# TensorE's order in a period of stage 1: the two fp32 products of a unit placed one on each side of the first tile's six products

## The chip, the cores and the metric

The kernel is one program on one core of a Trainium2 chip. TensorE does the matrix products, VectorE (DVE), ScalarE (ACT) and GpSimd (POOL) the work on elements, and SyncE (SP) issues the transfers between device memory and on-chip memory. The engines run side by side, each through its own instructions in the order written, and wait for each other at semaphores. The metric is the device time of one execution in microseconds (us). The median of three executions of the kernel before is 848.15 us (848.12 to 851.08).

## The reference

Two layers, one behind the other, for 32 sequences b of 128 channels and 2048 time steps:

```python
# layer 1: a session's own two-layer network, masked by channel and by length
W = W_sess[session_ids];  b = b_sess[session_ids]          # 128 x 256 for each sequence
h = einsum('bct,bch->bht', x * cmask, W) + b[:, :, None]
h = gelu(h)                                                # 256 hidden rows: two tiles of 128
out = (einsum('bht,hs->bst', h, W2) + b2) * tmask
# layer 2: a product in fp8, quantized with the largest magnitudes of out and of weight
w_q = fp8_e4m3(weight * w_scale);  x_q = fp8_e5m2(out * x_scale)
y = einsum('bsk,nk->bsn', x_q, w_q) / x_scale / w_scale + bias
return x + y
```

`x_scale` needs the largest magnitude of the whole `out`, so layer 2 can't begin before layer 1 has ended.

## The kernel before

The work has two stages. Stage 1 computes layer 1 for 64 units (half a sequence each: 128 channels x 1024 steps) and stores `out` to device memory; beside it the weight (128 x 32768 numbers) is scanned for its maximum (units 0 to 19) and later scaled, rounded and kept on chip in chunks of 768 columns. Stage 2 reads `out` back, quantizes it and makes the large product, 64 matmuls a sequence. The change touches stage 1 alone.

The hidden layer of a unit u has two tiles of 128 rows. Its precision comes from splitting: `xh` is x rounded to the fp32r format and `xl` the rest, `whl` holds the session weight's two parts, and `hidden(u, t)` (lines 698 to 722) makes tile t out of three products (weight high x `xh`, weight low x `xh`, weight high x `xl`), each in two halves of 512 columns: six matmuls, of one record each. `hidden(u, 0)` writes the first half of the tensor `ps_h` and `hidden(u, 1)` the second. Tile 0's output layer is split in the same way: `project0` (line 724) makes six matmuls of `w2h`, `w2l` with `hh` and `hl`. Tile 1's is `project1` (line 733): two products of unsplit fp32, one for each half, of which each has two records in the trace. Both add into `ps_o[:, u % 2]`.

The other engines, per unit, each in this order:

- ScalarE in its iteration u: `split_x(u + 2)` (line 448, writes `xh`), `gelu0(u + 1)` (lines 454 and 455: the gelu of tile 0 twice, once rounded into `hh`, once in place), in units 22 to 64 `scale_chunk` (line 471), `gelu1(u + 1)` (line 460, writes `h1`), and for 28 odd u `mask_session_weight` (line 478, writes `whl` for a later sequence). `split_x(u + 2)` waits until `hidden(u, 1)` has ended, `gelu0(u + 1)` until `hidden(u + 1, 0)` has, and `gelu1(u + 1)` until `hidden(u + 1, 1)` has.
- VectorE in its iteration u: `mask_o(u - 1)` (lines 567 and 570: bias and time mask out of `ps_o`, then the maximum), two operations on a weight chunk (lines 581 and 583) or, earlier, one part of the weight's scan (line 589), and `split_h_rest(u + 1)` (line 557: `hl`, what `hh` has left of the gelu), which stands ahead of the scan.
- GpSimd: `xl` (line 406), then the two rounding operations of a chunk (lines 413 and 415).

TensorE's order is written out by hand (lines 740 to 765). Its waits matter here: `hidden(u + 1, 0)` overwrites the half of `ps_h` that `hl` of unit u is computed from, so it waits for `hl_ready` of unit u. `hidden(u + 1, 1)` overwrites what `gelu1(u)` reads, and waits for `h1_gelu` of unit u, as the fp32 products do, which read `h1`. Every product into `ps_o` waits until VectorE has emptied that buffer two units earlier (`o_masked`).

Of the kernel before, what the change touches and what calls it, by code (L numbers as in the profile page):

```python
# [6 lines left out]
def adaln_ffn(nc, x, ids, lens, counts, w_sess, b_sess, w2, b2, weight, bias, out, masked_out, split_w):  # L7
# [8 lines left out]
    P = 128  # L16
    B, C, T = x.shape
    NSESS, _, HID = w_sess.shape
    HT = HID // P
    F = b2.shape[0] * 16  # L20
# [34 lines left out]
    HALVES = [slice(0, BANK), slice(BANK, UNIT)]  # L55
# [7 lines left out]
    with ExitStack() as ctx:  # L63
        def sb(name, shape, dt):
            return ctx.enter_context(nc.sbuf_tensor(name, shape, dt))

        def sem(name):
            return ctx.enter_context(nc.semaphore(name))
# [15 lines left out]
        w2_sb = sb("w2_sb", [P, HT, P], fp32)  # L84
        w2h = sb("w2h", [P, P], fp32r)
        w2l = sb("w2l", [P, P], fp32r)
# [21 lines left out]
        hh = sb("hh", [P, 2, UNIT], fp32r)  # L108
        hl = sb("hl", [P, 2, UNIT], fp32r)
        h1 = sb("h1", [P, 2, UNIT], fp32)  # L110
# [36 lines left out]
        ps_o = ctx.enter_context(nc.psum_tensor("ps_o", [P, 2, UNIT], fp32))  # L147
# [36 lines left out]
        h1_gelu = sem("h1_gelu")  # L184
        hl_ready = sem("hl_ready")
        o_psum = sem("o_psum")
        o_masked = sem("o_masked")
# [49 lines left out]
        def h0_of(u):  # L237

            return ps_o[:, 1, :] if u == 1 else ps_h[:, 0, :]
# [440 lines left out]
        def _(pe):  # L680
# [9 lines left out]
            def hidden_bias():  # L690
                pe.wait_ge(bs_loaded, 16)
                pe.wait_ge(onehot_ready, 1)
                for t in range(HT):
                    last_mm = nc.tensor.matmul(ps_o[:, 0, t * B:(t + 1) * B], bs_sb[:, t * P:(t + 1) * P],
                                               onehot[:, :], start=True, stop=True)
                last_mm.then_inc(hbias_psum, 1)

            def hidden(u, t):
                b = u // UPB
                to = h0_of(u) if t == 0 else ps_h[:, 1, :]  # L700
                if t == 0:
                    if u % UPB == 0:
                        if b < DIRECT:
                            pe.wait_ge(wh_direct, b + 1)
                        else:
                            pe.wait_ge(whl_masked, b - DIRECT + 1)
                    pe.wait_ge(xh_ready, u + 1)

                    if u > 1:
                        pe.wait_ge(hl_ready, u)  # L710
                elif u > 0:
                    pe.wait_ge(h1_gelu, u)
                for k, (part, xs) in enumerate(((0, xh), (1, xh), (0, xl))):
                    rows = slice(part * HID + t * P, part * HID + (t + 1) * P)
                    if k == 1 and t == 0 and b < DIRECT and u % UPB == 0:
                        pe.wait_ge(wl_direct, b + 1)
                    if k == 2 and t == 0:
                        pe.wait_ge(xl_ready, u + 1)
                    for cols in HALVES:
                        mm = nc.tensor.matmul(to[:, cols], whl[:, b % DIRECT, rows], xs[:, u % 2, cols],  # L720
                                              start=(k == 0), stop=(k == 2))
                mm.then_inc(h0_psum if t == 0 else h1_psum, 1)

            def project0(u, halves):

                pe.wait_ge(hl_ready, u + 1)
                if u >= 2:
                    pe.wait_ge(o_masked, u - 1)
                for k, (w, hs) in enumerate(((w2l, hh), (w2h, hh), (w2h, hl))):
                    for cols in halves:  # L730
                        nc.tensor.matmul(ps_o[:, u % 2, cols], w[:, :], hs[:, u % 2, cols], start=(k == 0), stop=False)  # L731

            def project1(u, halves):
                pe.wait_ge(h1_gelu, u + 1)
                for cols in halves:
                    mm = nc.tensor.matmul(ps_o[:, u % 2, cols], w2_sb[:, 1, :], h1[:, u % 2, cols],  # L736
                                          start=False, stop=True)
                mm.then_inc(o_psum, 1)

            hidden_bias()  # L740
            hidden(0, 0)
            hidden(0, 1)
# [2 lines left out]
            for u in range(UNITS - 2):  # L745
                if u > 0:
                    hidden(u + 1, 0)
                if u == SCANS + 2:

                    pe.wait_ge(scale_step, 1)  # L750
                project0(u, HALVES)
                if u == SCANS + 1:
                    pe.wait_ge(w_pmax_ready, 1)
                    nc.tensor.matmul(w_row, w_pmax, ident_f[:, :], start=True, stop=True).then_inc(w_row_psum, 1)
                hidden(u + 1, 1)
                project1(u, HALVES)
                if u == SCANS + 1:
                    pe.wait_ge(w_one_ready, 1)
                    nc.tensor.matmul(w_all, ones[:, :], w_one[:, :], start=True, stop=True).then_inc(w_amax_psum, 1)
# [22 lines left out]
            for k in range(CUTS):  # L782
                pe.wait_ge(q_ready, k + 1)
                pe.sem_inc(identity_turn, 1)
                for j in range(k * KT // CUTS, (k + 1) * KT // CUTS):
                    mm = nc.tensor.matmul(ps_q[:, j * P:(j + 1) * P], q_by_pair[:, 0, j // 2, :, j % 2], ident[:, :],
                                          start=True, stop=True)
# [50 lines left out]
```

## Time and profile before

| | |
|---|---|
| median of three executions | 848.15 us |
| profiled execution, its time | 847.79 us |
| its span, first to last instruction | 846.0 us |
| stage 1, until the last fp32 product | about 392 us |
| TensorE busy in the span | 832.6 us (98%) |
| TensorE busy at line 720, 731, 736 (stage 1) and 804 (stage 2) in the chain that ended last | 19%, 10%, 12% and 50% of the span |
| ScalarE, VectorE, GpSimd busy in the span | 320.1, 479.9, 444.2 us |
| TensorE's granted clock | 1.0 of full speed throughout |

In the profile's rows PE is a matmul on TensorE, PEld its weight load, which can run beside another matmul, and L720 a line of the kernel. Starts count from the first instruction. The end of a matmul is modelled, so lengths are better read from one start to the next. A bracket at the end of a row gives how long the engine had been idle before it and who released it.

### The profile page before, as it was taken

The numbers are of one execution on the slowest core, as the hardware profiler recorded it, in microseconds if no ns is written. First come the engines' busy times: TensorE is split into PE (matmuls) and PEld (weight loads), VectorE is DVE, ScalarE is ACT, GpSimd is POOL, SyncE is SP. The second block draws the span as 40 slices with busy tenths as digits, with TensorE's granted clock in tenths as the row PEclk, the third lists the DMA queues.
The fourth block names the chain that finished last, engine by engine and source line by source line (L and its number), as shares of the span: only waits on it lengthen the run. The fifth ranks groups of instructions, "written<-read, shape, count | busy, mean of one in ns | idle before, by whom it ended". The sixth has DMA issues, their size and how long they took to land.

```text
span 846.0 us, 9980 instructions
## 1 busy us (share of the span) xinstructions
PE 832.6 (98%) x3467; PEld 471.2 (56%) x3502; DVE 479.9 (57%) x495; ACT 320.1 (38%) x334; POOL 444.2 (53%) x195
## 2 busy tenths in 40 slices
PE   7999999999999999999999999999999999999998
PEld 4767676767767676675444444444444444444443
DVE  6889998888888888888532323232323232332322
ACT  5767777889888898884000000000000000000000
POOL 3634343799999999996632333323242424242321
PEclk9999999999999999999999999999999999999999
DMA  7799997676768866655569686867677676768672
GB/s 272 289 374 421 354 350 277 241 291 256 299 256 340 337 254 246 260 221 212 201 203 282 215 280 215 279 211 273 225 258 242 242 258 225 277 213 285 217 248 100
DMA packets 73022, 222.06 MB, mean 262 GB/s; under 512 B 37402, under 2 KB 39202, under 8 KB 52642
## 3 DMA queue, kind: packets, MB, share of 16 engines
q1 hardware_dynamic: 72994, 221.71, 73.1%
q8 instruction: 15, 0.25, 0.1%
q14 instruction: 13, 0.11, 0.0%
HBM read 144.35 MB, written 69.21 MB: 252 GB/s over the span
## 4 chain that ended last, share of the span: by engine, by line
PE 91%; DMA 3%; DVE 3%; issue 1%; POOL 1%; SPq 1%; ACT 1%; DVEq 0%
PE ps_h L804 50%; PE ps_h L720 19%; PE ps_o L736 12%; PE ps_o L731 10%; DMA split_w<-wqT 1%; DMA lens_i<-in_itok_B 1%; DVE hl L557 0%; DMA wraw<-split_w 0%; DMA x_sb<-x_sb 0%; DVE whl L523 0%; DVE x_sb L647 0%; DVE o_sb L567 0%; SPq L263 0%; POOL xl L406 0%; DVE wc L583 0%
## 5 line engine op out<-in xcount | busy, mean ns | idle before, releaser
L804 PE MATMUL ps_h<-wqT,x_sb 128*128 128x512 bf16 x2014 | 440.8, 379 | 2.7 <-DMA x_sb<-x_sb 0.8
L804 PEld LDWEIGHTS ps_h<-wqT,x_sb 128*128 128x128 fp8e5 x2048 | 200.1, 98 | 242.9 <-issue 2.2
L406 POOL TENSOR_TENSOR xl<-x_sb,xh 128x1024 fp32r<-128x1024 f32 x62 | 149.5, 2411 | 85.5 <-ACT xh L448 85.5
L720 PE MATMUL ps_h<-xh,whl 128*128 128x512 f32 x508 | 159.8, 436 | 3.6 <-DVE hl L557 2.4
L430 POOL TENSOR_TENSOR h<-h,bias_sb 128x2048 f32<-128x2048 f32 x16 | 73.3, 4579 | 139.0 <-DMA h<-in_x 139.0
L430 POOL TENSOR_TENSOR x_sb<-x_sb,bias_sb 128x2048 f32<-128x2048 f32 x16 | 72.3, 4519 | 139.9 <-DMA x_sb<-in_x 139.9
L670 DVE SCALAR_TENSOR_TENSOR o_sb<-ps_h,scales,h 128x512 f32<-128x512 f32 x64 | 48.0, 751 | 155.2 <-PE ps_h L804 155.2
L670 DVE SCALAR_TENSOR_TENSOR o_sb<-ps_h,scales,x_sb 128x512 f32<-128x512 f32 x64 | 47.8, 750 | 145.1 <-PE ps_h L804 145.1
L720 PEld LDWEIGHTS ps_h<-xh,whl 128*128 128x128 f32 x508 | 96.1, 190 | 51.6 <-issue 31.1
L736 PE MATMUL ps_o<-h,w_sb 128*128 128x512 f32 x256 | 120.3, 592 | 0.0
L567 DVE SCALAR_TENSOR_TENSOR o_sb<-ps_o,b_sb,steps 128x1024 f32<-128x1024 f32 (+1 forms) x65 | 82.2, 1265 | 32.0 <-PE ps_o L736 31.8
L454 ACT ACTIVATE hh<-ps_h,hbias 128x1024 fp32r<-128x1024 f32 x63 | 70.7, 1122 | 50.0 <-PE ps_h L720 50.0
L557 DVE TENSOR_TENSOR hl<-ps_h,hh 128x1024 fp32r<-128x1024 f32 x63 | 76.7, 1218 | 12.2 <-ACT ps_h L455 12.2
L720 PE MATMUL ps_h<-xl,whl 128*128 128x512 f32 x254 | 79.8, 395 | 0.0
L570 DVE TENSOR_REDUCE o_max<-o_sb 128x1 f32<-128x1024 f32 (+1 forms) x65 | 78.3, 1204 | 2.3
L460 ACT ACTIVATE h<-ps_h,hbias 128x1024 f32<-128x1024 f32 x64 | 71.3, 1114 | 17.0 <-PE ps_h L720 17.0
L413 POOL TENSOR_TENSOR ws<-ws,wc 128x768 f32<-128x768 f32 (+1 forms) x43 | 70.4, 1637 | 12.2 <-DVE wc L583 10.8
L415 POOL TENSOR_TENSOR wqT<-ws,wc 128x768 bf16<-128x768 f32 (+1 forms) x43 | 71.1, 1653 | 3.4
L736 PEld LDWEIGHTS ps_o<-h,w_sb 128*128 128x128 f32 x256 | 48.3, 189 | 36.2 <-issue 30.6
L455 ACT ACTIVATE ps_h<-ps_h,hbias 128x1024 f32<-128x1024 f32 x63 | 67.9, 1078 | 0.0
L448 ACT ACTIVATE xh<-x_sb 128x1024 fp32r<-128x1024 f32 x62 | 65.7, 1059 | 0.0
L720 PEld LDWEIGHTS ps_h<-xl,whl 128*128 128x128 f32 x254 | 48.1, 190 | 11.5 <-DVE xl L540 0.3
(79 smaller groups left out, 452.9 us busy)
## 6 DMA issues: line engine op xcount, KB each, us to landing
x_sb<-in_x SPq DMA_DIRECT2D x47, 1024.0 KB, 5.2
masked_out<-o_sb SPq DMA_DIRECT2D x32, 1024.0 KB, 5.4
o_in<-masked_out SPq DMA_DIRECT2D x32, 1024.0 KB, 8.9
out<-o_sb SPq DMA_DIRECT2D x31, 1024.0 KB, 5.1
h<-in_x SPq DMA_DIRECT2D x16, 1024.0 KB, 7.1
wt<-in_L_ffn_weight SPq DMA_DIRECT2D x42, 384.0 KB, 5.4
wqT<-in_L_ffn_weight SPq DMA_DIRECT2D x19, 832.0 KB, 8.1
wraw<-split_w SPq DMA_DIRECT2D x28, 256.0 KB, 5.0
```

Source lines behind the costliest of these rows:

```text
L406: pool.tensor_tensor(xl[:, u % 2, :], x_cols(u), xh[:, u % 2, :].bitcast(fp32), ALU.subtract)\
L415: pool.tensor_tensor(wqT[:, CHUNK_AT[i]], v, c, ALU.subtract).then_inc(w_rounded, 1)
L430: pool.tensor_tensor(x2[r], x2[r], bias_sb[:, :], ALU.add).then_inc(xb_ready, 1)
L460: act.activation(h1[:, u % 2, :], ps_h[:, 1, :], ACT.Gelu, bias=hbias[:, 1, b:b + 1])\
L557: dve.tensor_tensor(hl[:, u % 2, :], h0_of(u), hh[:, u % 2, :].bitcast(fp32), ALU.subtract)\
L567: dve.scalar_tensor_tensor(o_cols(u)[:, cols], ps_o[:, u % 2, cols], b2_sb[:, :], window, ALU.add, ALU.mult)\
L570: dve.tensor_reduce(o_max[:, u + k:u + k + 1], o_cols(u)[:, cols], AX.X, ALU.max, apply_absolute_value=True)\
L670: dve.scalar_tensor_tensor(y_sb[:, r, cols], ps_y[n], y_scale, x2[r][:, cols], ALU.mult, ALU.add).then_inc(y_ready, 1)
L720: mm = nc.tensor.matmul(to[:, cols], whl[:, b % DIRECT, rows], xs[:, u % 2, cols], start=(k == 0), stop=(k == 2))
L731: nc.tensor.matmul(ps_o[:, u % 2, cols], w[:, :], hs[:, u % 2, cols], start=(k == 0), stop=False)
L736: mm = nc.tensor.matmul(ps_o[:, u % 2, cols], w2_sb[:, 1, :], h1[:, u % 2, cols], start=False, stop=True)
L804: mm = nc.tensor.matmul(ps_y[n], qT[:, r, k // 2, :, k % 2], wq[:, n, k, :], start=(k == 0), stop=(k == KT - 1))
```

## The change

Inside the loop over the units, `project0` and `project1` are no longer called. The first fp32 product (`first_half`) now stands ahead of tile 0's six output products (`project`), the second (`second_half`) right behind them, and `hidden(u + 1, 1)` comes last in the loop's body. The wait for `h1_gelu` of unit u moves with the first fp32 product, and `ps_o` is started by it in its first half. The last two units, behind the loop, still call the old functions.

```diff
+            def first_half(u):
+                pe.wait_ge(h1_gelu, u + 1)
+                if u == 1:
+                    pe.wait_ge(hl_ready, u + 1)
+                if u >= 2:
+                    pe.wait_ge(o_masked, u - 1)
+                nc.tensor.matmul(ps_o[:, u % 2, HALVES[0]], w2_sb[:, 1, :], h1[:, u % 2, HALVES[0]], start=True, stop=False)
+
+            def project(u):
+                pe.wait_ge(hl_ready, u + 1)
+                for k, (w, hs) in enumerate(((w2l, hh), (w2h, hh), (w2h, hl))):
+                    for h, cols in enumerate(HALVES):
+                        mm = nc.tensor.matmul(ps_o[:, u % 2, cols], w[:, :], hs[:, u % 2, cols], start=(h == 1 and k == 0),
+                                              stop=(h == 0 and k == 2))
+                return mm
+
+            def second_half(u):
+                nc.tensor.matmul(ps_o[:, u % 2, HALVES[1]], w2_sb[:, 1, :], h1[:, u % 2, HALVES[1]], start=False, stop=True)\
+                  .then_inc(o_psum, 1)
...
-                project0(u, HALVES)
+                first_half(u)
+                project(u)
                 if u == SCANS + 1:
                     pe.wait_ge(w_pmax_ready, 1)
                     nc.tensor.matmul(w_row, w_pmax, ident_f[:, :], start=True, stop=True).then_inc(w_row_psum, 1)
+                second_half(u)
                 hidden(u + 1, 1)
-                project1(u, HALVES)
```

On TensorE in stage 1, one body of the loop of the kernel before, from the six products of `project0` to the next body's `hidden`. `w_sb` is W2 with `h` the array `h1`; L720 into `ps_h` is `hidden`, with one row for each wait:

```order
L731 MATMUL ps_o<-hh,w2l 128x512 [waits o_masked,hl_ready]
L731 MATMUL ps_o<-hh,w2l 128x512
L731 MATMUL ps_o<-hh,w2h 128x512 x2
L731 MATMUL ps_o<-hl,w2h 128x512 x2
L720 MATMUL ps_h<-xh,whl 128x512 [waits h1_gelu]
L720 MATMUL ps_h<-xh,whl 128x512 x3
L720 MATMUL ps_h<-xl,whl 128x512 x2
L736 MATMUL ps_o<-h,w_sb 128x512 [waits h1_gelu]
L736 MATMUL ps_o<-h,w_sb 128x512
L720 MATMUL ps_h<-xh,whl 128x512 [waits hl_ready,xh_ready,wh_direct]
```

The same stretch in the changed kernel, where L749 is `first_half`, L755 `project` and L761 `second_half`:

```order
L749 MATMUL ps_o<-h,w_sb 128x512 [waits o_masked,h1_gelu]
L755 MATMUL ps_o<-hh,w2l 128x512 [waits hl_ready]
L755 MATMUL ps_o<-hh,w2l 128x512
L755 MATMUL ps_o<-hh,w2h 128x512 x2
L755 MATMUL ps_o<-hl,w2h 128x512 x2
L761 MATMUL ps_o<-h,w_sb 128x512
L720 MATMUL ps_h<-xh,whl 128x512 [waits h1_gelu]
L720 MATMUL ps_h<-xh,whl 128x512 x3
L720 MATMUL ps_h<-xl,whl 128x512 x2
L720 MATMUL ps_h<-xh,whl 128x512 [waits hl_ready,xh_ready,wh_direct]
```

The two `hidden` now follow each other: the one that waits for `hl_ready` (the next body's tile 0) comes directly behind the one whose end lets ScalarE go on, and the first fp32 product, with its wait for `h1_gelu`, follows six matmuls later. `o_psum` is signalled ahead of `hidden(u + 1, 1)`, not behind it. The counts of matmuls are the same; ScalarE, VectorE, GpSimd and SyncE have the same instructions in the same order.

## Rows read from the trace of the kernel before

**Rows 1.** Two stretches of stage 1: us, busy us of PE, PEld, DVE, ACT, POOL, clock.

```profile
30.00:130.00 100.00, 98.98 (x370) 69.28 (x369) 90.92 (x68) 73.91 (x75) 42.06 (x20) 1.00 0.95 367
150.00:390.00 240.00, 240.00 (x897) 168.27 (x896) 204.95 (x203) 209.56 (x222) 224.58 (x120) 1.00 0.72 271
```

**Rows 2.** The waits from 60 to 390: total us, times, longest us.

```profile
ACT hh L454 <- PE ps_h L720: 41.1, 56, 1.9
DVE o_sb L567 <- PE ps_o L736: 31.4, 40, 1.3
```

**Rows 3.** The chain that ended last, two periods: start us, us, what.

```profile
64.12 1.39 PE ps_h L720 x6
65.50 1.40 PE ps_o L731 x6
...
68.29 1.72 PE ps_o L736 x4
70.00 1.39 PE ps_h L720 x6
```

**Rows 4.** Timeline of a regular period: start us, us, then the instruction.

```profile
62.24 1.88 PE L736 MATMUL ps_o<-h,w_sb 128*128 128x512 f32 x4
62.44 1.11 ACT L460 ACTIVATE h<-ps_h,hbias 128x1024 f32<-128x1024 f32 x1 [0.69 <-PE ps_h L720]
...
63.45 0.71 ACT L478 ACTIVATE whl<-wraw,cmask 128x512 fp32r<-128x512 f32 x1
...
64.07 1.05 ACT L448 ACTIVATE xh<-x_sb 128x1024 fp32r<-128x1024 f32 x1
...
65.34 0.63 PE L731 MATMUL ps_o<-hh,w2l 128*128 128x512 f32 x2
65.54 1.12 ACT L454 ACTIVATE hh<-ps_h,hbias 128x1024 fp32r<-128x1024 f32 x1 [0.42 <-PE ps_h L720]
...
67.67 1.23 DVE L557 TENSOR_TENSOR hl<-ps_h,hh 128x1024 fp32r<-128x1024 f32 x1 [0.20 <-ACT ps_h L455]
...
68.56 0.19 PEld L736 LDWEIGHTS ps_o<-h,w_sb 128*128 128x128 f32 x1 [0.24 <-issue]
```

**Rows 5.** Timeline at the stall behind the first masked session weight.

```profile
52.95 0.72 ACT L478 ACTIVATE whl<-wraw,cmask 128x512 fp32r<-128x512 f32 x1 [2.41 <-DMA wraw<-split_w]
...
53.58 1.05 ACT L448 ACTIVATE xh<-x_sb 128x1024 fp32r<-128x1024 f32 x1
...
54.53 1.09 ACT L454 ACTIVATE hh<-ps_h,hbias 128x1024 fp32r<-128x1024 f32 x1
...
55.52 1.08 ACT L455 ACTIVATE ps_h<-ps_h,hbias 128x1024 f32<-128x1024 f32 x1
...
56.63 1.23 DVE L557 TENSOR_TENSOR hl<-ps_h,hh 128x1024 fp32r<-128x1024 f32 x1 [2.41 <-ACT ps_h L455]
...
58.01 1.16 PE L720 MATMUL ps_h<-xh,whl 128*128 128x512 f32 x4 [1.02 <-DVE hl L557]
...
59.00 0.39 PE L720 MATMUL ps_h<-xl,whl 128*128 128x512 f32 x1
```

**Rows 6.** Timeline of the last unit, where TensorE waits for a gelu.

```profile
389.10 0.63 PE L731 MATMUL ps_o<-hh,w2l 128*128 128x512 f32 x2
389.29 1.12 ACT L460 ACTIVATE h<-ps_h,hbias 128x1024 f32<-128x1024 f32 x1 [1.55 <-PE ps_h L720]
...
390.46 0.30 PEld L736 LDWEIGHTS ps_o<-h,w_sb 128*128 128x128 f32 x2 [0.24 <-ACT h L460]
...
391.00 0.19 PEld L736 LDWEIGHTS ps_o<-h,w_sb 128*128 128x128 f32 x1 [0.24 <-issue]
```

**Rows 7.** Line 478: count, duration ns (min/median/max), first and last start.

```profile
L478 ACT ACTIVATE whl<-wraw,cmask x28: 711/726/730, 52.9 to 371.0; 128x512 fp32r<-128x512 f32 x28
```

**Rows 8.** Timeline of GpSimd, one period while the weight is rounded.

```profile
202.38 2.42 POOL L406 TENSOR_TENSOR xl<-x_sb,xh 128x1024 fp32r<-128x1024 f32 x1
...
208.31 2.41 POOL L406 TENSOR_TENSOR xl<-x_sb,xh 128x1024 fp32r<-128x1024 f32 x1
```

## The prediction

> **What bounds the kernel now.** I read the busy times by stretch first, then the waits, the chain that ended last, and the timeline of one period. In stage 1 TensorE is never idle from 150 to 390 us, while ScalarE is busy 209.56 of 240 us, VectorE 204.95 and GpSimd 224.58 [rows 1]. The others wait for TensorE, 41.1 us at the gelu of tile 0 and 31.4 us at `mask_o`, and these are the longest waits; none of TensorE's is in that list [rows 2]. The chain stays on TensorE: six `hidden` matmuls in 1.39 us, six output products in 1.40, six more of `hidden` in 1.39 (66.90 to 68.29), four records of the two fp32 products in 1.72; from 64.12 to 70.00 a period is 5.88 us [rows 3]. So the stage is a stream of matmuls, with other engines close behind. Two questions decide: can the new order shorten the stream, and does it bring in a wait that the old one covered?
>
> **The stream itself.** Eighteen matmuls of 1.39/6 = 0.232 us and four records of 0.43 us are there before and after. Were the two fp32 products costly because they stand together, splitting them would pay. But the records follow each other at 0.43 us, and the loads between them end early: the load engine sits idle 0.24 us before the next [rows 4]. The single records of `hidden` and of the output products cost the same 0.232 us wherever they stand [rows 3]. I take 0 for this. The bounds: if a record behind an fp32 product could be as short as half an fp32 record, 0.215 us, each would gain 0.017. One more such place in 62 periods is -1.1 us, and if all six behind it gained, -6.5 us. If each new boundary instead cost what one exposed load costs, 0.43 - 0.24 = 0.19 us, it would be +12; the first record behind the fp32 products today shows nothing of it, since the period adds up without it (4.17 + 1.72 = 5.89).
>
> **The wait for the gelu of tile 1.** Call E the moment at which a `hidden` of tile 1 ends and the next matmul begins. Before, the next `hidden` of tile 1 was the first to need that gelu, more than 4 us later. Now `hidden(u + 1, 0)` alone stands between, 1.40 us. The trace has this very arrangement once, in the last unit, with six output products between: they begin at 389.10, which is E, the gelu starts at 389.29, and the load of the fp32 product starts at 390.46, released by that gelu; the second record's load, and so the second record, starts at 391.00, which puts the first at 390.57 [rows 6]. That is E + 1.47, against E + 1.40 without a wait: 0.08 us for each unit in which nothing else is late.
>
> **The wait for `hl`.** This is the larger term. `hidden(u + 1, 0)` needs `hl` of unit u. Let E be the end of `hidden(u - 1, 1)`, behind which `hidden(u, 0)` follows. From there ScalarE runs in order: gelu of tile 1 of u - 1, on half of the units the masked session weight, `split_x`, then the two gelus of tile 0 of u; VectorE follows with `hl`. Before, the fp32 products and `hidden` stood between E and the start of gelu 0, so it started at 65.54 for an E of 62.24, 3.30 us, and the three ScalarE entries ahead of it were through by then (it idled 0.42 us) [rows 4]. Its `hl` ended at 67.67 + 1.23 = 68.90, while the matmul that needed it came at 62.24 + 1.72 + 5.88 = 69.84: 0.7 us of slack even after the release. Now `hidden` of tile 0 ends 1.40 + 0.20 = 1.60 after E, ScalarE's queue ahead of gelu 0 is longer than that, and the matmul that needs `hl` comes one period after E, at 5.88, not 7.60.
>
> The length of this chain is in the trace, link by link. E to the gelu of tile 1: 62.24 to 62.44, 0.20. To the next entry: 63.45, 1.01 [rows 4]. From the masked weight's start to the matmul that `hl` releases, with nothing else in between, 52.95 to 58.01; that first record is stretched, since four of them end at 59.00, so that the true start is 59.00 - 4 x 0.232 = 58.07: 5.12 [rows 5]. The sum is 6.33 us after E. Without the masked weight (63.45 to 64.07, 0.62 [rows 4]) it is 5.71.
>
> Against a period of 5.88, 5.71 is in time. 6.33 is not. So take two units: from the E behind which the mask stands, the start of `hidden` of tile 0 that needs this `hl` is at 6.33, and from there the next E of the same kind is one undisturbed period on, 5.88: 12.21 for two, against 11.76, +0.45. The 0.08 of the first unit lies inside the 6.33; in the second unit the gelu of tile 1 starts 0.37 us ahead of the late matmul and is ready. There are 28 masked weights, 52.9 to 371.0 [rows 7]. The first is the stall of the kernel before, in which it waited 2.41 us for its transfer; there the same chain runs today, so the changed kernel loses nothing and comes out of it at the same 58 us, whatever it lost earlier. That leaves 27 pairs: 27 x 0.45 = 12.2 us.
>
> **What else is moved.** `o_psum` comes 1.4 us earlier relative to the next `hidden`, so VectorE begins `mask_o` earlier and has slack for it; it is no gain, because TensorE's wait for `o_masked` was never late. Once, in unit 21, the small product for the weight's scale stands between the two fp32 ones: its wait keeps the second fp32 product back as it kept `hidden` back before; I take 0, within 0.3 either way. GpSimd has 5.93 us of work and waits in a period while it rounds (202.38 to 208.31) [rows 8], and the period grows to 6.1, so it gains slack. SyncE's transfers are behind releases that move by less than a unit; x is needed two units after. The last two units and stage 2 have their old order. A TensorE stall of 0.37 us is shorter than the 1.02 us one at 58 us, through which the clock stayed at 1.00 [rows 1, 5]. Sum: +12.2 on the profiled execution's 847.8 (span 846.0 and 1.8 around it) is 860.0. The median of the runs shown is 0.4 above that execution: 860.4.
>
> **Rivals.**
>
> *A, the loads hide the waits and the stream shrinks (faster).* For it: the load engine is idle 0.24 us behind each fp32 record [rows 4]. If loads ran more than one product ahead, the second boundary in a period would pay, 1.1 to 6.5 us, and stalls would be partly absorbed: 842 to 847, say 844. Against it: the load behind a wait starts only 0.05 us after the gelu has ended (390.41 to 390.46) [rows 6], so it isn't ahead of its wait. It decides from the point where a load starts two products early. The Trainium skill, "TensorE: Matmul & The Clock Gate", section "Architectural detail: the array is 16× 32×32, not 1× 128×128", gives TensorE a queue 64 deep with a partial reorder window that pulls weight loads ahead of matmuls in flight. By that rule the loads could be through at every release and this rival's 844 would hold; in these rows a load starts behind its release and no earlier.
>
> *B, only the short wait shows.* If VectorE or ScalarE get through the queue faster than in the stalled case, `hl` is in time and the 0.08 us remains: 54 x 0.08 = 4.3, 852.4. For it: the margin that I find late is 0.45 of 6.33. Against: each link is measured.
>
> *C, no wait at all.* ScalarE's queue is hidden, as it was: 848.1. Against it, the arithmetic of 1.60 against 1.01 + 0.62 + 0.95 us of queue.
>
> *D, a second engine joins (slower still).* While the weight is rounded ScalarE has `scale_chunk` ahead of the gelu of tile 1, and that needs a buffer that GpSimd frees. GpSimd has 224.58 of 240 us of work [rows 1]. `xl` now starts later after a masked weight. If GpSimd falls behind by 0.3 us in half of the 43 chunk units, the gelu of tile 1 and all behind it are late: about +6 us, 866. It decides once GpSimd's work per period passes 6.1 us; it is at 5.93 with its waits.
>
> **How the numbers follow.** Forecast 0.72, D 0.12, B 0.07, C 0.05, A 0.04. The forecast's own range, from 0.05 us of error in each chain length (27 x 0.1 = 2.7) and 0.3 to 1 us of edges, is 857 to 864. The range reaches to B's upper part and to D: 853 to 867. A measurement of this kernel tells about 0.5% (4.2 us) from no change. Faster by more: A's far end, 0.03. Within: C, half of B and the near end of A, 0.09. Slower: 0.88.
>
> **What would show it.** Right: the period alternates, about 5.96 and 6.25 us, from 64 us on; TensorE waits some 27 times about 0.3 to 0.4 us at line 720 for line 557, and shortly at line 749 for line 460; ScalarE's gelu of tile 0 is no longer idle before it, but its idle time stands before the gelu of tile 1; the stream of the other records keeps 0.232 and 0.43. Wrong: waits of `hidden` in every unit (chain longer than 5.9 without the mask), in none (B or C), a release by GpSimd (D), or records shorter than 0.23 behind the fp32 products (A).

## Result and profile after

The changed kernel takes 863.16 us (median of 5; 862.29 to 864.26) against 848.15 us before (median of 5): 1.0166 times as long, with a 95% interval of 1.0147 to 1.0186. The forecast was 860.4, within 853 to 867. The profiled execution took 863.33 us, 15.5 more than that of before.

Lines of the page of the changed kernel (busy time of each engine; TensorE's granted clock in 40 slices; two groups, with the idle time ahead of them):

```profile
PE 843.4 (98%) x3467; PEld 467.8 (54%) x3502; DVE 479.1 (56%) x495; ACT 317.3 (37%) x334; POOL 442.1 (51%) x195
...
PEclk9989999999999999999999999999999999999999
...
L557 DVE TENSOR_TENSOR hl<-ps_h,hh 128x1024 fp32r<-128x1024 f32 x63 | 77.0, 1222 | 53.2 <-ACT ps_h L455 52.9
...
L460 ACT ACTIVATE h<-ps_h,hbias 128x1024 f32<-128x1024 f32 x64 | 71.5, 1117 | 79.8 <-PE ps_h L720 79.8
```

VectorE now idles 52.9 us for the gelus of tile 0, 12.2 before, and ScalarE 79.8 us ahead of the gelu of tile 1, 17.0 before. The busy share of TensorE says nothing of this: 98% both times, because the modelled end of a matmul covers a late start.

The waits of the changed kernel from 60 to 400 us (total, times, longest):

```profile
POOL xl L406 <- ACT xh L448: 81.2, 36, 8.7
ACT h L460 <- PE ps_h L720: 65.7, 55, 4.0
DVE hl L557 <- ACT ps_h L455: 45.9, 33, 3.2
PEld ps_h L720 <- issue: 39.9, 137, 0.5
...
PEld ps_o L749 <- ACT h L460: 7.0, 27, 0.3
...
PE ps_h L720 <- DVE hl L557: 2.8, 1, 2.8
ACT hh L454 <- PE ps_h L720: 2.4, 1, 2.4
```

Against [rows 2]: both waits shown there are gone. ScalarE's gelu of tile 0 waited 56 times for TensorE and now does once, while its gelu of tile 1 waits 55 times; VectorE no longer waits for `ps_o`, but for the gelu of tile 0. The longest in total is GpSimd's, for `xh`, as it was before (58.5 us, 17 times, from 60 to 390 us). The first fp32 product waits 27 times for the gelu of tile 1. The 27 waits for `hl` are not listed as such; they stand in the load engine's "issue". They must be read from starts. The timeline of one pair of units:

```profile
92.63 1.09 PE L720 MATMUL ps_h<-xh,whl 128*128 128x512 f32 x4
92.83 1.12 ACT L460 ACTIVATE h<-ps_h,hbias 128x1024 f32<-128x1024 f32 x1 [2.21 <-PE ps_h L720]
...
93.84 0.71 ACT L478 ACTIVATE whl<-wraw,cmask 128x512 fp32r<-128x512 f32 x1
94.00 0.30 PEld L749 LDWEIGHTS ps_o<-h,w_sb 128*128 128x128 f32 x2 [0.25 <-ACT h L460]
...
94.45 1.05 ACT L448 ACTIVATE xh<-x_sb 128x1024 fp32r<-128x1024 f32 x1
...
95.40 1.11 ACT L454 ACTIVATE hh<-ps_h,hbias 128x1024 fp32r<-128x1024 f32 x1
...
96.40 1.08 ACT L455 ACTIVATE ps_h<-ps_h,hbias 128x1024 f32<-128x1024 f32 x1
...
97.51 1.22 DVE L557 TENSOR_TENSOR hl<-ps_h,hh 128x1024 fp32r<-128x1024 f32 x1 [1.39 <-ACT ps_h L455]
...
98.88 1.17 PE L720 MATMUL ps_h<-xh,whl 128*128 128x512 f32 x4
...
99.89 0.62 PE L720 MATMUL ps_h<-xl,whl 128*128 128x512 f32 x2
```

E, where a `hidden` of tile 1 has ended and the next `hidden` of tile 0 begins, is 92.63. ScalarE works from 92.83 to 97.5 without a pause, through gelu, mask, `split_x` and two gelus. The following `hidden` of tile 0, which needs this `hl`, begins at 99.89 - 4 x 0.232 = 98.96, which is E + 6.33. The chain that ended last, in the same stretch (start us, us, what):

```profile
86.54 0.13 issue
86.67 1.62 PE ps_h L720 x6
88.29 0.86 PE ps_o L749 x2
89.15 1.40 PE ps_o L755 x6
...
91.41 2.76 PE ps_h L720 x12
...
98.88 1.17 PE ps_h L720 x4
```

From one late start to the next are 98.88 - 86.67 = 12.21 us for two units, against 2 x 5.88 in [rows 3]. Inside, the stream is the old one: 1.40 for six output products, 0.86 for each fp32 product.

The rest is at the start. Stretches of 2 us of the changed kernel (busy us and instructions of PE, PEld, DVE, ACT, POOL; granted clock; DMA share; GB/s):

```profile
58.00:60.00 2.00, 0.60 (x2) 0.53 (x3) 1.97 (x2) 1.97 (x2) 0.45 (x1) 0.65 1.04 281
60.00:62.00 2.00, 2.00 (x6) 1.61 (x5) 2.00 (x2) 0.00 (x0) 1.95 (x1) 0.50 0.96 372
...
64.00:66.00 2.00, 2.00 (x8) 1.56 (x7) 1.54 (x2) 0.43 (x1) 0.00 (x0) 0.64 1.05 427
```

and its timeline there:

```profile
54.35 0.72 ACT L478 ACTIVATE whl<-wraw,cmask 128x512 fp32r<-128x512 f32 x1 [2.61 <-DMA wraw<-split_w]
...
59.40 2.05 PE L720 MATMUL ps_h<-xh,whl 128*128 128x512 f32 x4 [2.83 <-DVE hl L557]
...
68.20 1.08 PE L720 MATMUL ps_h<-xh,whl 128*128 128x512 f32 x4
```

The first masked weight begins 1.40 us later than in [rows 5], at 54.35. TensorE is idle 2.83 us, up to 59.40; by the mean of 0.65 from 58 to 60 us the granted clock falls within this idle time to 0.50, the 1.2 GHz level, and it stays there until past 65 us. The next `hidden` of tile 0 starts at 68.20; in the kernel before it was 58.07 + 5.88 = 63.95. So 4.25 us are lost by then.

### The profile page after: what moved, and what is told of

Read it like the earlier page. It is cut to its first block, busy times and chain, and to the rows that moved or that the text cites. A ratio compares the mean times of both kernels' runs of the same rounds, so it can differ in the third digit from the quotient of the medians.

```text
span 861.6 us, 9981 instructions
## 1 busy us (share of the span) xinstructions
PE 843.4 (98%) x3467; PEld 467.8 (54%) x3502; DVE 479.1 (56%) x495; ACT 317.3 (37%) x334; POOL 442.1 (51%) x195
## 4 chain that ended last, share of the span: by engine, by line
PE 89%; DMA 3%; DVE 3%; ACT 2%; issue 2%; POOL 1%; SPq 1%; DVEq 0%; ACTq 0%
PE ps_h L829 50%; PE ps_h L720 19%; PE ps_o L755 9%; PE ps_o L749 6%; PE ps_o L761 5%; DMA split_w<-wqT 1%; DVE hl L557 1%; DMA lens_i<-in_itok_B 1%; ACT xh L448 1%; DMA wraw<-split_w 1%; ACT ps_h L455 0%; ACT hh L454 0%; DMA x_sb<-x_sb 0%; DVE x_sb L647 0%; PE ps_o L731 0%
## 5 line engine op out<-in xcount | busy, mean ns | idle before, releaser
L406 POOL TENSOR_TENSOR xl<-x_sb,xh 128x1024 fp32r<-128x1024 f32 x62 | 148.1, 2388 | 107.1 <-ACT xh L448 107.1
L720 PE MATMUL ps_h<-xh,whl 128*128 128x512 f32 x508 | 167.8, 453 | 7.3 <-DVE hl L557 4.1
L720 PEld LDWEIGHTS ps_h<-xh,whl 128*128 128x128 f32 x508 | 94.8, 192 | 63.0 <-issue 48.9
L557 DVE TENSOR_TENSOR hl<-ps_h,hh 128x1024 fp32r<-128x1024 f32 x63 | 77.0, 1222 | 53.2 <-ACT ps_h L455 52.9
L460 ACT ACTIVATE h<-ps_h,hbias 128x1024 f32<-128x1024 f32 x64 | 71.5, 1117 | 79.8 <-PE ps_h L720 79.8
L720 PE MATMUL ps_h<-xl,whl 128*128 128x512 f32 x254 | 79.4, 394 | 0.0
L455 ACT ACTIVATE ps_h<-ps_h,hbias 128x1024 f32<-128x1024 f32 x63 | 68.2, 1082 | 0.0
L749 PE MATMUL ps_o<-h,w_sb 128*128 128x512 f32 x124 | 67.4, 625 | 0.1
L755 PE MATMUL ps_o<-hh,w2l 128*128 128x512 f32 x124 | 64.5, 602 | 1.0 <-DVE hl L557 1.0
L761 PE MATMUL ps_o<-h,w_sb 128*128 128x512 f32 x124 | 63.5, 593 | 0.0
```

The source lines that it names most:

```text
L406: pool.tensor_tensor(xl[:, u % 2, :], x_cols(u), xh[:, u % 2, :].bitcast(fp32), ALU.subtract)\
L557: dve.tensor_tensor(hl[:, u % 2, :], h0_of(u), hh[:, u % 2, :].bitcast(fp32), ALU.subtract)\
L749: nc.tensor.matmul(ps_o[:, u % 2, HALVES[0]], w2_sb[:, 1, :], h1[:, u % 2, HALVES[0]], start=True, stop=False)
L755: mm = nc.tensor.matmul(ps_o[:, u % 2, cols], w[:, :], hs[:, u % 2, cols], start=(h == 1 and k == 0), stop=(h == 0 and k == 2))
L761: nc.tensor.matmul(ps_o[:, u % 2, HALVES[1]], w2_sb[:, 1, :], h1[:, u % 2, HALVES[1]], start=False, stop=True)\
```

## Experiments

Two theories stood against each other. **Q**: ScalarE's queue makes `hl` late, because the two `hidden` follow each other. **S**: the separation of the fp32 products costs it in TensorE's stream. A third, **A**, was that separation shortens the stream.

### 1. The fp32 products together, `hidden` of tile 1 last

An edit of the kernel before:

```diff
+                project1(u, HALVES)
                 hidden(u + 1, 1)
-                project1(u, HALVES)
```

> The two fp32 products stand together again, as before, and only hidden(u + 1, 1) is moved behind them, to the end of the body. Theory Q (ScalarE's queue and the wait for hl cost the time, because the two hidden now follow each other): the chain from the end of hidden of tile 1 to the next hidden of tile 0 that needs hl is the same 6.33 us with a masked weight, against a period of 5.89, so 27 pairs cost 0.44 each and the start costs what it cost in the changed kernel: 860 to 865. Theory S (the separation of the fp32 products costs it, by switches in the matmul stream): 847 to 850.

Measured: 862.86 us (862.07 to 863.29, 4 runs), 1.0173 times the kernel before (1.0156 to 1.019). That is the whole slowdown, with the two fp32 products still together. From 66 to 388 us its waits (total, times, longest) have the changed kernel's form, without those for `h1`:

```profile
ACT h L460 <- PE ps_h L720: 63.0, 53, 3.5
DVE hl L557 <- ACT ps_h L455: 41.8, 29, 1.8
...
PE ps_h L720 <- DVE hl L557: 5.2, 25, 0.2
```

Theory S falls. The last row names the wait that the prediction had priced, 25 times: `hidden` for `hl`. Here the chain that ended last leaves TensorE once in each pair of units and runs through ScalarE's queue (start us, us, what):

```profile
91.89 0.71 ACT whl L478
92.60 0.95 ACT xh L448
93.55 1.00 ACT hh L454
94.55 0.98 ACT ps_h L455
...
95.56 1.24 DVE hl L557
...
96.93 1.62 PE ps_h L720 x6
```

### 2. Apart, with `hidden` of tile 1 ahead of the second fp32 product

An edit of the changed kernel:

```diff
+                hidden(u + 1, 1)
                 second_half(u)
-                hidden(u + 1, 1)
```

> The fp32 products stay apart, one on each side of the six output products, but hidden(u + 1, 1) stands ahead of the second one, so that 0.86 us lie between the two hidden again. Theory Q: hl is needed 5.89 + 0.86 = 6.74 us after the end of hidden of tile 1, later than the 6.33 of the longest chain, so no wait in mid-stage, and the stream of matmuls has the same length: 847.5 to 850. Theory S: as slow as the changed kernel, 860 to 865. Rival A of the prediction (standing apart shortens the stream): 842 to 847.

Measured: 849.14 us (847.18 to 853.69, 12 runs), 1.0008 times before (0.9987 to 1.0029): no change that can be measured. The fp32 products are as far apart as in the changed kernel. The 0.86 us that lie between the two `hidden` are enough, as 6.74 against 6.33 said. Its chain (start us, us, what) is TensorE's stream alone:

```profile
157.24 0.86 PE ps_o L749 x2
...
159.50 1.37 PE ps_h L720 x6
160.88 0.86 PE ps_o L761 x2
161.73 1.38 PE ps_h L720 x6
163.12 0.86 PE ps_o L749 x2
```

A period is 163.12 - 157.24 = 5.88; by the unrounded starts of the trace it is 5.873 in nearly every unit, where the kernel before has 5.887. So there is a gain of the smallest size that A allowed, 0.014 us a period, 0.9 us in all. That it comes from the separation is not shown: in experiment 1, where nothing is separated, the periods without a wait are 5.880, half of the way. In the profiled execution it is outweighed, since this kernel lost 3.2 us more than before at the first masked weight, part of it at a clock of 0.79 (58 to 66 us).

### 3. The changed kernel with the masked weight later in ScalarE's order

```diff
                 if u + 1 < UNITS:
                     gelu0(u + 1)
+                if u % UPB == 0 and DIRECT <= (u + 2) // 2 < B:
+                    mask_session_weight((u + 2) // 2)
...
-                if u % UPB == 1 and DIRECT <= (u + 3) // 2 < B:
-                    mask_session_weight((u + 3) // 2)
```

> The changed kernel with the masked session weight moved in ScalarE's order, from behind the gelu of tile 1 to behind the two gelus of tile 0 of the next unit, where ScalarE idles. Theory Q: every chain is 5.71 us, in time; the period is 5.97 everywhere (the 0.08 of the wait for the gelu of tile 1 shows alone), 54 x 0.08 = 4.3 over the kernel before, and at the start the late transfer of the first masked weight no longer blocks the gelus: 851.5 to 855. If the waits for hl had another cause than the masked weight in ScalarE's queue: 860 to 864, with the alternation 5.87 / 6.34 still there.

Measured: 853.29 us (850.72 to 855.66, 4 runs), 1.0068 times before (1.0046 to 1.009), and so 9.9 us less than the changed kernel, by medians; these four runs lie 4.9 us apart. The alternation is gone; the loads that wait for `h1` come in every unit:

```profile
81.79 0.30 PEld L749 LDWEIGHTS ps_o<-h,w_sb 128*128 128x128 f32 x2 [0.27 <-ACT h L460]
...
90.54 0.72 ACT L478 ACTIVATE whl<-wraw,cmask 128x512 fp32r<-128x512 f32 x1
...
93.71 0.30 PEld L749 LDWEIGHTS ps_o<-h,w_sb 128*128 128x128 f32 x2 [0.27 <-ACT h L460]
```

Two units lie between the two loads, so (93.71 - 81.79)/2 = 5.96: the 0.08 of the wait for the gelu of tile 1, now in every unit (52 times in its list of waits), and nothing else. The masked weight at 90.54 costs nothing where it stands. Without the alternation 27 pairs are up to 27 x (12.21 - 2 x 5.96) = 7.8 us shorter (the periods are 5.95 to 6.00); the rest of the gain is at the start, where the gelus no longer stand behind the transfer of the first masked weight.

### 4. The changed kernel with TensorE kept busy at the first masked weight

```diff
+                if u == 7:
+                    pe.wait_ge(o_masked, 6)
+                    for k in range(3):
+                        nc.tensor.matmul(ps_o[:, 1, 0:BANK], time[:, 0:P], time[:, 0:BANK], start=True, stop=True)
                 if u > 0:
                     hidden(u + 1, 0)
```

> The changed kernel with three fp32 matmuls of the warm-up kind (0.86 us each, results never used) ahead of hidden(8, 0), where TensorE idles at the first masked weight and its clock then falls to half. Theory K (the clock costs 2.8 us there): the granted clock stays at 1.00 in 58 to 66 us and the time falls by 2 to 3.5 us, to 859.5 to 861.5. Theory L (only the later transfer costs, and the clock's share is small): 862.5 to 864.

Measured: 861.10 us (860.87 to 861.80, 4 runs), 1.0152 times before (1.0134 to 1.0169), 2.1 us under the changed kernel, whose five runs all lie above these four. In the profiled execution the clock stays up (columns as above):

```profile
58.00:60.00 2.00, 1.29 (x4) 0.25 (x2) 1.40 (x2) 2.00 (x3) 1.02 (x1) 1.00 1.04 291
60.00:62.00 2.00, 2.00 (x9) 1.51 (x9) 2.00 (x2) 0.93 (x2) 1.37 (x1) 1.00 0.99 368
```

In 60 to 62 us it has nine matmuls where the changed kernel has six. Useless matmuls in a gap make the kernel faster, so the half clock was a cost of its own. The first masked weight was no earlier than in the changed kernel (54.92 against 54.35).

### 5. The masked weight made twice for 17 sequences

```diff
+                    sp.wait_ge(whl_masked, 19)
                     load_o(r, r)
...
+                if DIRECT < b < 22:
+                    act.wait_ge(whl_masked, b - DIRECT)
+                    act.activation(o_in[:, 1, 0:2 * HID], wraw[:, b % 2, :], ACT.Copy, scale=cmask[:, b:b + 1])
                 act.activation(whl[:, b % DIRECT, :], wraw[:, b % 2, :], ACT.Copy, scale=cmask[:, b:b + 1])\
```

The first line keeps the loads of `out` for stage 2 away from the place that the copy is written to.

> The changed kernel in which ScalarE makes the masked session weight twice for 17 of the 28 sequences (b = 5 to 21), the first time into a place that nobody reads. One of them takes 0.61 us of ScalarE's queue. Theory Q: the chain from the end of hidden of tile 1 to the hidden that needs hl becomes 6.33 + 0.61 = 6.94 in those pairs, and nothing else in them has slack to give: +0.61 x 17 = 10.4 over the changed kernel, 872 to 875. If the masked weight were not on the path (something else of every second unit is): 863 to 865.

Measured: 873.13 us (872.79 to 874.37, 4 runs), 1.0283 times before (1.0256 to 1.031), and 10.0 over the changed kernel, where 10.4 was expected. One pair in its timeline (line numbers are 4 higher for TensorE and VectorE here, L482 is the masked weight, ahead of it stands its double):

```profile
94.77 1.08 PE L724 MATMUL ps_h<-xh,whl 128*128 128x512 f32 x4
...
96.60 0.71 ACT L482 ACTIVATE whl<-wraw,cmask 128x512 fp32r<-128x512 f32 x1
...
101.64 1.16 PE L724 MATMUL ps_h<-xh,whl 128*128 128x512 f32 x4 [0.72 <-DVE hl L561]
...
102.64 0.62 PE L724 MATMUL ps_h<-xl,whl 128*128 128x512 f32 x2
```

From 94.77 to 101.64 are 6.87, and to the true start, 102.64 - 4 x 0.232 = 101.71, 6.94: the 6.33 and the 0.61 of the second copy, undiminished. With the wait this long, the row does name its releaser.

### 6. The kernel before with the masked weight later

The same edit as in experiment 3, on the kernel before.

> The kernel before with the masked session weight moved in ScalarE's order as in the third experiment. Mid-stage never waited, so only the one stall at 58 us is at stake, 7.13 - 5.89 = 1.25 us: ScalarE no longer stands behind a transfer there. Theory Q: 846.5 to 847.5, with no period over 5.95 between 25 and 130 us. Otherwise (the hidden that needs that weight waits for it just as long): 848.2.

Measured: 846.39 us (845.42 to 848.42, 12 runs), 0.9972 times before (0.9959 to 0.9985). It is the fastest version here, though by 1.8 us only, and 0.1 us faster than the range expected. In its trace the stall of 1.02 us in [rows 5] has shrunk to 0.40, although the transfer landed later:

```profile
51.28 1.89 DVE L589 TENSOR_REDUCE w_max<-wqT 128x1 f32<-128x1664 f32 x1 [1.79 <-DMA wqT<-in_L_ffn_weight]
...
54.43 0.72 ACT L478 ACTIVATE whl<-wraw,cmask 128x512 fp32r<-128x512 f32 x1 [0.31 <-DMA wraw<-split_w]
...
56.88 1.17 PE L720 MATMUL ps_h<-xh,whl 128*128 128x512 f32 x4 [0.40 <-DVE hl L557]
```

But the claim that no period would pass 5.95 was wrong: three are 6.52, 5.98 and 6.44, which is 1.28 us over 3 x 5.887, as much as the 1.25 of the one long period before. The new delays come from VectorE. It waited 1.79 us for a transfer of the scan (51.28), and `mask_o` and `hl` stood behind that. The profiled execution is only 0.4 us faster than that of before, and its first period (from the output products of unit 0 to those of unit 1), ahead of any masked weight, is 0.9 us shorter (6.57, before 7.52). So where the 1.8 us of the medians come from is not shown.

### 7. Experiment 2's order with the masked weight later

Both edits together.

> The second experiment's order (fp32 products apart, hidden of tile 1 ahead of the second) with the masked weight moved in ScalarE's order. The second experiment showed periods of 5.873 against 5.887 and lost 3.2 us at the first masked weight. Theory Q: the periods stay 5.873, which is 62 x 0.014 = 0.9 us, and the stall and the half clock at the start go: 848.15 - 1.25 - 0.9 = 846.0, between 845.3 and 846.8. If the stall at the start has another cause: 849.

Measured: 846.95 us (845.62 to 849.19, 12 runs), 0.9975 times before (0.9958 to 0.9993); 846.0 was expected, and the result is 0.15 outside that range. Its periods in mid-stage are 5.873. The profiled execution, of 848.6, gave the gain back at the start: VectorE waited 2.6 us for a transfer of the scan and so made `hl` late, for which TensorE waited up to 2.0 us, and the clock was 0.91 in 12 to 30 us. From experiment 6 it cannot be told apart: the 0.9 us of the shorter period is below what the start varies by.

## Why the prediction held, and where it was off

**The stream: right, to 0.9 us.** Taken as 0; experiments 1 and 2 show that separation costs nothing. The period of experiment 2 is 0.014 us shorter, 0.9 us in all, near the first bound of -1.1 (for the second bound, 62 x 6 x 0.017 is 6.3, not 6.5).

**The wait for `hl`: right.** The 6.33 was read link by link before the change and is 6.33 in the changed kernel (92.63 to 98.96). A pair is 12.21, as forecast; its two periods are 5.97 and 6.24 by the starts of the output products. Experiment 5 lengthens the chain by 0.61 and gets 0.61, experiment 3 takes the masked weight out of it and the alternation goes, experiment 2 moves the deadline by 0.86 and it goes as well. With 5.887 for a period in place of the 5.88 of the rounded rows, 27 pairs are 27 x 0.44 = 11.9 us.

**The wait for the gelu of tile 1: right.** 0.08 a unit, visible alone in experiment 3, whose period is 5.96, and hidden inside the 6.33 in the changed kernel.

**The start: wrong, by more than the 2.8 us that the forecast missed.** The step was that the changed kernel "comes out of it at the same 58 us", and that the clock stays at 1.00 through a stall there. It came out 4.25 us late: 1.40 because the first masked weight's transfer landed later, and the other 2.85 between 59.4 and 68.2, where the clock was halved. The prediction looked only at stalls of 0.37 us, and took this one over from the old trace as it stood. Here TensorE idled 2.83 us in place of 1.02: 1.40 for the later transfer, and 0.4 because it had come to the wait earlier (by its rows it had been idle since 59.40 - 2.83 = 56.57, before since 58.01 - 1.02 = 56.99). Experiment 4 gets back 2.1 of it with the clock held. Whether the later transfer is due to the change stays open. The masked weight, released by its transfer, starts at 52.95 in the trace of before, at 54.43 in experiment 6, which has the old order on TensorE, and at 53.98 to 55.66 in experiments 1, 2, 4 and 5. Of the 1.40 us, 0.33 lie ahead of the transfer's issue (49.56 before, 49.89 changed) and 1.07 behind it; from the issue to the masked weight are 3.39 us before, 4.46 in the changed kernel and 4.40 in experiment 6. So 52.95 was the early one, and my working, tied to one trace's transfer, had no margin for that.

**The scale in unit 21: outside its 0.3.** The term was 0, "within 0.3 either way". Two extra delays of 0.67 and 0.51 before (periods of 6.56 and 6.39 for 5.89) became one of 0.66, so -0.5. The sum is 4.25 + 11.9 - 0.5 = 15.6, against 15.5 between the profiled executions. The result lies inside 857 to 864, the forecast's own range, but that range was made for errors in the chain's length (2.7 us) and for edges (0.3 to 1 us). The chain had no such error, the start had 4.25; that it fitted into the room left for others is luck.

**A list misread.** The prediction calls the waits for TensorE the longest. The list of waits that it read has a longer one, GpSimd's for `xh`, 58.5 us from 60 to 390; nothing hangs on it, since GpSimd's `xl` was not late for TensorE there.

**The rivals.** B and C are excluded by the alternation. D did not come: GpSimd waits longer than before for `xh` (107.1 us in the page, 85.5 before) and its rounding holds up ScalarE no more than before (3.5 us over the whole kernel, before 4.1). A's mechanism, loads that run ahead, is not in the trace: the load behind the gelu's wait starts at 94.00, not before the gelu's end at 93.95.

## What to carry to other kernels

Where an engine writes two buffers in turn and others empty them, the distance between the two producers is slack for the queue between them. Before closing it up, add the in-order entries of the engine that serves both, from the first producer's end to the consumer that frees the other buffer, and compare with the period, with every optional entry in it. An entry that can be late without harm belongs behind the urgent ones. Here the masked weight is needed by the same `hidden` that waits for `hl` (98.96), but by itself it is ready at 93.84 + 0.71 = 94.55, while four more operations are still to come for `hl`. Behind the gelus of tile 0 it runs beside VectorE's `hl`, at 90.54 in experiment 3, where ScalarE would idle: in the changed kernel that was worth 9.9 us. In the kernel before it was worth 1.8, of which the trace does not show where.

## What the runs showed of the hardware

- Idle times of nearly the same length did not have the same effect on TensorE's clock. In stalls of 2.83 us in the changed kernel, 3.8 in experiment 5 and 2.6 in experiment 2 the granted clock fell to 0.50, for about 7, 7 and 3.5 us; in one of 3.2 us in experiment 1 it stayed at 1.00, and in the 1.02 of the kernel before too. It also differs between executions of one kernel: over the whole of experiment 1's profiled execution the mean clock was 1.000, over its three others 0.996 or 0.997 (where it fell in those is not recorded). A stall of that size can cost as much again, 2.85 us for 2.83 in the changed kernel, or nothing.
- An fp32 record of 512 columns takes 0.43 us and an fp32r one 0.23 in any order tried, and changes between them cost nothing measurable: the period with two such changes more (experiment 2) is 0.014 us shorter.
- About the first quarter of a us of a wait for a semaphore does not show as idle time of the matmul rows, whose modelled ends reach past it. The 0.37 us of the changed kernel show not at all, the 0.45 of experiment 1 as 0.2, the 0.98 of experiment 5 as 0.72. The rest is in the load engine, partly as "issue", and in the distance between starts.
